# Scan layer of a four-layer kernel: softplus in one ScalarE function, both silus together, dt rows stored earlier, steps written out

## The reference

```python
xz = xs @ W_in
xi, z = jnp.split(xz, 2, axis=-1)                    # 64 channels each
xc = silu(causal_conv(xi, conv_w, taps=4) + conv_b)
dbl = xc @ W_x
dt_r, Bc, Cc = jnp.split(dbl, [dtr, dtr + d_state], axis=-1)   # dtr 2, d_state 16
dt = jax.nn.softplus(dt_r @ W_dt + b_dt)
A = -jnp.exp(A_log)
def step(h, inp):
    x_t, dt_t, B_t, C_t = inp
    dA = jnp.exp(dt_t[:, :, None] * A)
    h = dA * h + dt_t[:, :, None] * B_t[:, None, :] * x_t[:, :, None]
    y = jnp.einsum('bds,bs->bd', h, C_t)
    return (h, y)
y = yT + xc * D_skip
return (y * jax.nn.silu(z)) @ W_out
```

## Time and profile before

| what | value |
|---|---|
| median of three runs | 3129.49 us (3125.74 to 3132.32) |
| span of the profiled execution | 3123.6 us |
| scan layer in it | from 1254.6 us on; first scan at 1295.61 us |
| busy in the whole span | PE 82%, DVE 80%, POOL 66%, ACT 61% |
| busy in 57 us of the scan layer | DVE 55.98, POOL 50.03, PE 48.55, ACT 42.37 us |
| instructions | 40760 |

### The profile page before, as it was taken

One profiled execution on the slowest core, in us unless ns is written; L12 is line 12 of the kernel. 1 busy time (PEld: TensorE's weight loads), 2 busy tenths in 40 slices (PEclk: granted clock), 3 DMA queues, 4 the chain that ended last, 5 costly groups with the idle time before them and its releaser, 6 DMA issues.

```text
span 3123.6 us, 40760 instructions
## 1 busy us (share of the span) xinstructions
PE 2573.1 (82%) x12954; PEld 756.1 (24%) x12954; DVE 2485.6 (80%) x2176; ACT 1914.4 (61%) x2402; POOL 2065.3 (66%) x1284
## 2 busy tenths in 40 slices
PE   5888878888788775688888888888888888888886
PEld 1233123331233211222222222222222222222221
DVE  5655656555555544599999999999999999999998
ACT  4534654346543343667777777677777776777772
POOL 2543245432444313298898888988988889889886
PEclk9999999999999988799999999999999999999999
DMA  4797327863279647667677677676775766767765
GB/s 162 241 325 212 102 67 255 294 205 102 72 241 313 192 133 181 132 146 181 147 165 167 144 177 163 148 181 148 162 170 145 179 160 148 180 148 162 171 145 117
DMA packets 257701, 537.53 MB, mean 172 GB/s; under 512 B 39608, under 2 KB 150656, under 8 KB 256688
## 3 DMA queue, kind: packets, MB, share of 16 engines
q1 hardware_dynamic: 215328, 444.01, 53.7%
q0 software_dynamic: 19040, 64.24, 7.7%
q10 hardware_dynamic: 23216, 27.74, 3.7%
HBM read 396.55 MB, written 139.33 MB: 172 GB/s over the span
## 4 chain that ended last, share of the span: by engine, by line
POOL 29%; issue 27%; PE 5%; DVE 2%; DMA 2%; ACT 1%; SPq 1%; POOLq 0%; ACTq 0%; DVEq 0%
POOL m_hs L500 18%; POOL m_sp_v L517 2%; POOL m_dtx L527 2%; POOL m_gated L506 2%; DMA t_tile<-band_out 1%; POOL m_dt L524 1%; POOL m_dt L520 1%; SPq L913 1%; DVE m_pb L472 1%; PE t_bank L1096 1%; PE t_bank L1057 1%; PE t_bank L1021 1%; POOL t_xc L1481 1%; DVE m_hs L477 1%; PE m_misc L230 0%
## 5 line engine op out<-in xcount | busy, mean ns | idle before, releaser
L500 POOL TENSOR_TENSOR m_hs<-m_hs,m_cs 128x1024 f32<-128x1024 f32 x512 | 1203.6, 2358 | 288.4 <-DVE m_hs L477 288.4
L477 DVE TENSOR_TENSOR_SCAN m_hs<-m_da,m_pb 128x1024 f32<-128x1024 f32 x512 | 1170.7, 2287 | 29.3 <-ACT m_da L399 4.2
L399 ACT ACTIVATE m_da<-m_dtb,m_a_neg 128x1020 f32<-128x1020 f32 x512 | 576.6, 1144 | 275.9 <-DMA m_dtb<-dt_rows 254.1
L282 PE MATMUL m_pb<-m_dtx,late 64*128 64x512 f32 x2048 | 583.5, 646 | 150.2 <-DVE m_hs L477 146.9
L265 PE MATMUL m_py<-m_hs,late 128*64 128x512 f32 x2048 | 565.8, 631 | 104.8 <-POOL m_hs L500 104.0
L472 DVE TENSOR_TENSOR m_pb<-m_pb,m_bs 128x1024 f32<-128x1024 f32 x512 | 619.7, 1210 | 20.9 <-PE m_pb L282 20.9
L1481 POOL TENSOR_TENSOR t_xc<-t_xc,big 128x512 f32<-128x512 f32 x96 | 120.1, 1271 | 338.8 <-DVE big L1387 338.8
L282 PEld LDWEIGHTS m_pb<-m_dtx,late 64*128 64x128 f32 x2048 | 163.4, 188 | 567.3 <-DVE m_hs L477 457.5
L1021 PE MATMUL t_bank<-late,t_lwin 128*128 128x256 f32 x816 | 217.3, 404 | 63.3 <-ACT big L1260 34.0
L1359 DVE SCALAR_TENSOR_TENSOR t_xc<-t_bank,t_vec,t_xc 128x512 f32<-128x512 f32 x96 | 72.0, 750 | 244.2 <-PE t_bank L1057 244.2
L1248 ACT ACTIVATE t_sq<-t_bank 128x512 f32<-128x512 f32 x192 | 105.5, 598 | 245.3 <-PE t_bank L1096 245.2
(11 more groups left out here) (166 smaller groups left out, 3591.3 us busy)
## 6 DMA issues: line engine op xcount, KB each, us to landing
m_dtb<-dt_rows SPq DMA_DIRECT2D x512, 512.0 KB, 6.1
late<-right_factor POOLq DMA_DIRECT2D x102, 512.0 KB, 5.5
right_factor<-t_tile SPq DMA_DIRECT2D x192, 256.0 KB, 3.5
t_tile<-band_out SPq DMA_DIRECT2D x183, 256.0 KB, 4.2
band_out<-t_vwin SPq DMA_DIRECT2D x48, 512.0 KB
band_out<-t_vwin SPq DMA_DIRECT2D x48, 480.0 KB
dt_rows<-m_dt ACTq DMA_DIRECT2D x64, 256.0 KB, 3.2
t_xc<-in_x_cm SPq DMA_DIRECT2D x4, 2048.0 KB, 14.6
```

Of the source, the lines that this page charges most:

```text
L282: m = nc.tensor.matmul(pb[s % 2][:, half(n)], spread[rows, dg, :], dtx[par][rows, half(q)], start=True, stop=True)
L399: nc.scalar.activation(da[:, s % DA_RING, :, 1:T], dtb[s % DTB_RING][:, :].rearrange("p (r t) -> p r t", t=T)[:, :, 1:T], ACT.Exp, scale=a ...
L477: nc.vector.tensor_tensor_scan(hs[:, s % H_RING, :], da[:, s % DA_RING, :, :].rearrange("p r t -> p (r t)"), pb[s % 2][:, :], 0.0, ALU.mul ...
L500: nc.gpsimd.tensor_tensor(hs[:, s % H_RING, :], hs[:, s % H_RING, :], cs[q][:, :], ALU.mult).then_inc(hc_ready, 1)
```

## The change

The chain of softplus on ACT and POOL becomes one ACT function that reads PSUM and writes `dt` in two halves, with a table of its own; the buffers and semaphores of the chain go. POOL keeps the product dt*x, at steps 9 and 10. PE makes x and z one behind the other at step 5 and dt at step 7, and ACT takes both silus at step 6, between two table loads, softplus at step 8, also between two, and stores the dt rows at step 9. bq1 and cq1 move up by one step on PE and on ACT. The waits of the stores and of SP's first load of a chunk change with that. The loop over the chunks is written out: all instructions of all chunks stand in the program, without registers.

```diff
-        FIRST_USE = {"x": 0, "dt": 1, "z": 2, "bq0": 3, "cq0": 4}
-        USE = {"x": 0, "bq1": 1, "cq1": 2, "dt": 3, "z": 4, "bq0": 5, "cq0": 6}
+        FIRST_USE = {op: i for i, op in enumerate(("x", "z", "dt", "bq0", "cq0"))}
+        USE = {op: i for i, op in enumerate(("bq1", "cq1", "x", "z", "dt", "bq0", "cq0"))}
...
         SHARES = {
-            "tensor": {0: [(PRE, "x")], 2: [(OWN, "bq1")], 4: [(OWN, "cq1")], 5: [(PRE, "dt")],
-                       8: [(PRE, "z"), (POST, "out")], 9: [(PRE, "bq0")], 11: [(PRE, "cq0")]},
+            "tensor": {1: [(OWN, "bq1")], 3: [(OWN, "cq1")], 5: [(PRE, "x"), (PRE, "z")], 7: [(PRE, "dt")],
+                       8: [(POST, "out")], 9: [(PRE, "bq0")], 11: [(PRE, "cq0")]},
...
-            "gpsimd": {5: [(POST, "gate1")], 13: [(OWN, "gate0")], 7: [(PRE, "loss0"), (PRE, "log0")], 8: [(PRE, "dt0"), (PRE, "loss1")],
-                       9: [(PRE, "log1"), (PRE, "dt1")], 10: [(PRE, "dtx0")], 11: [(PRE, "dtx1")]},
+            "gpsimd": {5: [(POST, "gate1")], 9: [(PRE, "dtx0")], 10: [(PRE, "dtx1")], 13: [(OWN, "gate0")]},
...
-            with eng.Fori(1, CHUNKS - 4, 2) as k:
-                chunk(k, 1, (NEXT2, PRE, OWN, POST))
-                chunk(k + 1, 0, (NEXT2, PRE, OWN, POST))
-            chunk(CHUNKS - 3, 1, (NEXT2, PRE, OWN, POST))
+            for k in range(1, CHUNKS - 2):
+                chunk(k, k % 2, (NEXT2, PRE, OWN, POST))
...
-                    elif op == "silu_x":
-                        if not early(k, 1):
-                            a.preload_act_table_set("silu_and_others")
+                    elif op == "silu":
+                        a.preload_act_table_set("silu_and_others")
...
-                        a.preload_act_table_set("natural_log_exp_and_others")
-                    elif op == "silu_z":
-                        a.preload_act_table_set("silu_and_others")
                         if not early(k, 2):
                             a.wait_ge(y_gated, 2 * k - 2)
...
-                    elif op in ("dt0", "dt1"):
-                        q = int(op[2])
-                        a.wait_ge(misc_ready[q], use(k, "dt") + 1)
+                    elif op == "dt":
+                        a.preload_act_table_set("softplus")
                         if not early(k, 1):
-                            a.wait_ge(dt_ready, 2 * k)
-                        nc.scalar.activation(sp_x[:, half(q)], misc[q][:, :], ACT.Identity, bias=b_dt).then_inc(misc_used[q], 1)
+                            a.wait_ge(dtx_ready, 2 * k)
+                            a.wait_ge(dt_stored[1 - par], stores_of(k - 1, 1 - par))
+                        for q in range(2):
+                            a.wait_ge(misc_ready[q], use(k, "dt") + 1)
+                            nc.scalar.activation(dt[:, half(q)], misc[q][:, :], ACT.Softplus, bias=b_dt).then_inc(misc_used[q], 1)
+                        a.preload_act_table_set("natural_log_exp_and_others")
                     elif op == "dt_rows":
-                        a.wait_ge(dt_ready, 2 * k + 2)
-                        if not early(k, 1):
-                            a.wait_ge(da_ready, S * k - DTB_RING + 1)
+                        for q in range(2):
+                            a.wait_ge(misc_used[q], use(k, "dt") + 1)
+                        if not early(k, 2):
+                            a.wait_ge(da_ready, S * (k - 1))
...
                     if s == 0:
                         sp.wait_ge(dt_stored[par], stores_of(k, par))
-                    elif not (first and s < DTB_RING):
+                    if not (first and s < DTB_RING):
                         sp.wait_ge(da_ready, g - DTB_RING + 1)
```

More of the change, by code:

```diff
@@ L149, in use @@
                 return FIRST_USE[name]
-            body = k if name in ("bq1", "cq1") else k - 1
-            if isinstance(k, int) and body == CHUNKS - 1:
-                return len(FIRST_USE) + len(USE) * body + ("bq1", "cq1").index(name)
+            body = k if name in OWN_USE else k - 1
+            if body == CHUNKS - 1:
+                return len(FIRST_USE) + len(USE) * body + OWN_USE.index(name)
             return len(FIRST_USE) + len(USE) * body + USE[name]
@@ L171, in mamba_layer, with schedule @@
         FIRST_X = {"vector": {13: [(NEXT2, "xg0")], 15: [(NEXT2, "xg1")]}}
[L172 to L180 removed]
+        FIRST = {"vector": {9: [(PRE, "dtx0"), (PRE, "dtx1")]}, "gpsimd": {}}
+        def schedule(name, pre, steps, post):
             def share(k, par, kinds, s):
[L183 removed]
+                table = FIRST if kinds == (PRE,) and k == -1 and name in FIRST else FIRST_X if k == -2 and name in FIRST_X else SHARES
                 for kind, op in table[name].get(s, []):
@@ L295, in post @@
                     m.then_inc(o_ready, 1)
-                schedule(pe, "tensor", pre, steps, post)
+                schedule("tensor", pre, steps, post)
             @block.scalar
@@ L415, in post @@
                     for g in range(G):
-                        a.dma_start(out[:, bass.ds(SUB * k + g * NG, SUB), :],
+                        a.dma_start(out[:, SUB * k + g * NG:SUB * k + g * NG + SUB, :],
                                     fin[DM * g:DM * g + DM, :].rearrange("p (n t) -> p n t", n=SUB)).then_inc(stored, 16)
-                schedule(a, "scalar", pre, steps, post)
+                schedule("scalar", pre, steps, post)
             @block.vector
@@ L511, in pre @@
                         return gate(k, par, 0)
[L512 to L529 removed]
+                    q = int(op[3])
+                    g_.wait_ge(misc_used[q], use(k, "dt") + 1)
+                    nc.gpsimd.tensor_tensor(dtx[par][:, half(q)], dt[:, half(q)], act[par][:, half(q)], ALU.mult).then_inc(dtx_ready, 1)
+                schedule("gpsimd", pre, steps, lambda k, par, op: gate(k, par, 1))
             @block.sync
@@ L543, in steps @@
                                  ).then_inc(dtb_loaded[s % DTB_RING], 16)
[L545 removed]
+                schedule("sync", None, steps, None)
                 sp.wait_ge(stored, 16 * G * CHUNKS)
```

107 lines of the change are left out of this document (13 added, 94 removed).

## The result

The changed kernel takes 3161.12 us (median of 4 runs, 3157.76 to 3167.22) where the kernel before takes 3129.97 beside it: a ratio of 1.0095, 95% interval 1.0073 to 1.0116. It is slower by 0.95%. The forecast was 3163.

A forecast was written before the change was run, and what follows sets the result against it. DVE was taken to bound the kernel, at a floor of 56.10 us a chunk. The terms -21.9 + 63.6 - 8.2 = +33.5 took the profiled span from 3123.6 to 3157.1 and the median to 3163 us, range 3148 to 3183.

The forecast's parts named there:

- What bounds the kernel: Scan layer: DVE sets the pace, with a floor of 56.10 us a chunk; steady chunks stand 56.80 apart.
- Points 1 and 5: Steady chunks: less work on POOL and ACT, and storing dt rows at step 9 instead of 14, each worth 0.
- Point 2: PE's step 0: with x gone, DVE's stall at step 1 and perhaps small pauses go, -21.9 us, at least -9.
- Point 3: PE's step 5: x and z together make DVE wait 2.05 us at step 6 in 31 chunks, +63.6 us (51.2 to 66.3).
- Point 4: ACT's silus and softplus: silu(z) newly waits for POOL's gate, but this and softplus stay covered, adding nothing.
- Point 6: Before the first scan: shorter softplus and earlier dt rows bring the first scan 8.2 us earlier (3.7 to 10.5).
- Sum: Whole kernel: -21.9 + 63.6 - 8.2 = +33.5 us, a median of 3163.
- A: PE's step 5: the chip hides x and z, leaving only the gains, 3099 us; 6%.
- B: PE's step 5 and the start: loss at its floor of 1.65 a chunk, start wins 10.5, 3148 us; inside the forecast's 78%.
- C: ACT late through softplus or POOL's gate: each us beyond the slack costs 31 us, 1 us late gives 3194; 12%.
- D: DVE's scans: small pauses stay, so x leaving step 0 gives only 9 to 13, 3172 to 3176 us; inside the forecast's 78%.

The follow-up runs named there:

- b_spread: Changed kernel with x halved over PE's steps 5 and 6, z at 7, dt at 9 and dependent work later: 3104.67 us, 0.9892 of the kernel before.
- d_soft_unroll: Kernel before with its loop written out and softplus by ACT's own function at step 6; x, z, store unmoved: 3124.56 us, 0.9956 of the kernel before.
- c_rows14: Changed kernel with the store of the dt rows back at ACT's step 14: 3161.29 us, 1.0096 of the kernel before.
- c_unroll: Kernel before with its loop over the chunks written out and nothing else: 3132.41 us, 0.9973 of the kernel before.
- c_gate6: Changed kernel with POOL's gate for the chunk before at POOL's step 6 instead of 5: 3373.99 us, 1.0759 of the kernel before.

## Why the prediction was right, point by point

- **What bounds the kernel** (DVE, 56.10 us a chunk at the floor): right. The changed kernel's last pitch is 56.10, and b_spread reaches 56.09 over 29 chunks.
- **Points 1 and 5** (freed engines and the earlier store are worth 0 in the steady part): right, by d_soft_unroll (0.02 us a chunk) and c_rows14 (0.00). The second holds with x at step 5. Where x stands at step 0, the late store does reach DVE now and then: DVE waits 1.55 us at 2771.69 in c_unroll and 1.67 at 2761.19 in d_soft_unroll, because ACT had waited over 9 us for the rows, made the input of the next chunk (`xg`) late, and PE stood idle between the halves of x (1.02 and 1.27 us).
- **Point 2** (x leaves step 0, -21.9): right in place; no idle is left at step 1, and with nothing in its place (b_spread) all of the 0.70 a chunk comes back, 0.13 of it by writing out the loop (c_unroll).
- **Point 3** (x and z together, 2.05 a chunk, +63.6): right in step, count and cause, too large by 0.2. From the multiply of step 4, I had x start at 2.21 and measured 2.20; x lasted 3.63 to z's start instead of 3.74; from z's start to DVE it was 2.90 instead of 3.08. The last has an overlap that I had not seen: a record of the matmul for DVE starts at 2066.88, before z's last one at 2067.31. So 8.73 instead of 9.03, late by 1.84; the pitch shows 1.87, since the multiply itself then takes 1.23 us instead of 1.21. Added up: 29 x 1.87 = 54.2, and 5.2 from the first scan to the first addition (93.48 us over 88.33, which is 25 steps of 3.445 and the 2.20 from a scan to the addition), 59.4 in place of 63.6. Of the 5.2, the waits behind x and z in chunks 0 and 1 are 2 x 1.87; the other 1.4 I had not foreseen.
- **Chunk 0** has these 1.4 us. It has two waits:

```profile
1306.66 1.23 DVE L409 TENSOR_TENSOR m_pb<-m_pb,m_bs 128x1024 f32<-128x1024 f32 x1 [0.57 <-PE m_pb L267]
...
1316.15 1.23 DVE L409 TENSOR_TENSOR m_pb<-m_pb,m_bs 128x1024 f32<-128x1024 f32 x1 [2.48 <-PE m_pb L267]
...
1296.00:1299.00 3.00, 1.89 (x4) 0.32 (x4) 2.97 (x2) 2.10 (x3) 2.29 (x1) 0.50 1.04 233
1299.00:1304.00 5.00, 4.74 (x8) 1.30 (x10) 4.93 (x5) 2.29 (x2) 3.63 (x2) 0.50 1.05 235
1304.00:1310.00 6.00, 6.00 (x25) 1.68 (x22) 5.40 (x3) 4.19 (x5) 3.46 (x2) 1.00 0.99 214
```

  In the two windows behind the first scan PE's granted clock is 0.50, and its matmul for DVE takes 2.08 us instead of 1.13. In the kernel before, the x matmuls of step 0 stand just ahead of the first scan, and the clock is 0.98 from 1290 to 1299 and 0.66 only in the five us after. From 3 to 9 us behind the first scan the clock is 0.50 in all seven kernels that have no x at step 0, while it is 0.72, 0.98 and 1.00 in the three that have it (before, c_unroll, d_soft_unroll). But c_unroll has a low stretch just ahead of that, with 0.57 from 1290 to 1299. That x left this place is a likely cause of the low clock there; no run took it apart from the rest of the start.
- **Point 4** (ACT is in time): right. silu(z) waits for POOL's gate, 4.03 us, and nobody waits for it; softplus takes 1.27 for two halves, which is the 0.69 a half taken, with the overlap that two silus have. I had drawn the time of a table load from the row and not from the Trainium skill (page "ScalarE: Activation LUTs", section "What ACT_TABLE_LOAD costs", a drain of 1.38 us on top of the load). The trace keeps to the row: two loads in a row start 1.29 us apart, and softplus starts 0.01 us after the second ends.
- **Point 6** (start, -8.2): measured -9.9. The step that failed is small: I let the store of the rows wait for the table load ahead of it, and its issue started 0.07 us after the load had (1281.53 and 1281.46), 1.2 us earlier. Most of the rest is silu(x), which ended 13.3 us into the layer where it had ended at 13.9. From bq0's copy to the first decay it is 9.34 us in both kernels, as taken.
- **Sum**: -21.9 + 59.4 - 9.9 = +27.6, and the layer grew by 27.5. The two errors, 4.2 us in point 3 and 1.7 in point 6, both made the forecast too slow, and the first would be 5.6 (31 x 0.18) without the 1.4 of chunk 0. The medians differ by 31.2 for 33.5. That they lie nearer to the forecast than the layer does is luck: 3.7 of the 31.2 us are not in the layer of the two profiles.
- **Rivals.** A's price was nearly right and its mechanism absent: PE does not hide x and z in one step, but where they are spread (b_spread) the layer is 31.8 us shorter than in the kernel before, for A's 30.1. B had the start nearly right (-10.5 for -9.9), but a chunk lost 1.87 and not 1.65. C's chain exists, with 1.25 us in hand by c_gate6. Beyond it a wait of 4.05 us cost 6.88 a chunk, more than the 31 us in all for each us that I gave it; whether a shorter wait would lower the clock too, no run shows. D did not come about.

## What to carry to other kernels

In an engine that works in order, next to the one that sets the pace, ask of each step not whether the engine is idle on average (PE here some 10 us in 57) but how much extra work fits between two deadlines, with what the steps around it carry over: the same six matmuls (twelve records) cost 1.87 us a chunk in one step and nothing in three. Taking work off engines that wait for the bound is worth its time only before the pipeline is full; here that start gave 9.9 us. Where a chain makes TensorE stand idle for some us in each round (4.86 in c_gate6), add the slower matmuls behind the idle to the price of the wait.
